# One exponential for two score banks in an attention and FP4 feed-forward kernel

## What is computed

```python
h = layernorm(x) * (1 + ca) + sa
q, k, v = h @ Wq + bq, h @ Wk + bk, h @ Wv + bv        # 16 heads of 16
scores = einsum('bhqd,bhkd->bhqk', q / 4, k) + 8 * rel_bias[bucket]
ctx = einsum('bhqk,bhkd->bhqd', softmax(scores), v)
x = x + ga * (ctx @ Wo + bo)
h = layernorm(x) * (1 + cb) + sb
x = x + gb * fp4_linear(silu(fp4_linear(h, w_gate)) * fp4_linear(h, w_up), w_down)
```

## Time and profile before

| | |
|---|---|
| median of three runs | 3792.81 us |
| lowest and highest | 3792.51 and 3795.49 us |
| span of the profiled execution | 3785.4 us |
| TensorE busy | 3473.1 us, 92% |
| TensorE weight loads | 2040.4 us |
| VectorE busy | 3208.1 us, 85% |
| ScalarE busy | 1872.9 us, 49% |
| GpSimd busy | 1696.3 us, 45% |
| mean granted TensorE clock | 0.968 |

### The profile page before, as it was taken

The page is one execution under the profiler, slowest core; times in us unless marked ns, Lnnn a source line. Parts: engine busy times, 40 slices in busy tenths (PEclk is TensorE's granted clock), DMA queues, the critical chain, the costliest instruction groups (busy, mean ns, idle before and its releaser), DMA issues.

```text
span 3785.4 us, 81397 instructions
## 1 busy us (share of the span) xinstructions
PE 3473.1 (92%) x22906; PEld 2040.4 (54%) x22906; DVE 3208.1 (85%) x7270; ACT 1872.9 (49%) x3800; POOL 1696.3 (45%) x1773
## 2 busy tenths in 40 slices
PE   1699999999999999999999999999999999999986
PEld 0245555555555555555555555555555555555554
DVE  7468888888888888888888888888888888888976
ACT  2265555545555455555554555555455545555541
POOL 2214544445454444444444445444445444444454
PEclk6799999999999999999999999999999999999997
DMA  3543323233332323332323432323333232333000
GB/s 98 97 83 70 73 50 67 50 65 74 73 62 59 58 54 73 75 73 50 67 46 69 74 72 59 59 56 60 72 73 65 60 55 53 73 75 66 20 22 12
DMA packets 199199, 237.30 MB, mean 63 GB/s; under 512 B 23424, under 2 KB 177568, under 8 KB 198736
## 3 DMA queue, kind: packets, MB, share of 16 engines
q1 hardware_dynamic: 198736, 231.64, 31.3%
HBM read 163.72 MB, written 67.31 MB: 61 GB/s over the span
## 4 chain that ended last, share of the span: by engine, by line
issue 46%; POOL 29%; PE 14%; DVE 6%; POOLq 2%; DMA 2%; SPq 1%; ACT 1%; DVEq 0%; ACTq 0%
POOL hidden L1250 5%; POOL hidden L1248 5%; PE ps_x L630 4%; POOL hidden L1274 4%; POOL parts L1219 3%; POOL proj L1212 3%; PE ps_o L618 2%; PE rings L581 2%; POOL ffn_in L1262 2%; POOL x_mid L1243 2%; POOL rstd L1260 2%; PE rings L597 1%; PE ps_x L656 1%; POOL hidden L1252 1%; POOLq L122 1%
## 5 line engine op out<-in xcount | busy, mean ns | idle before, releaser
L779 ACT ACTIVATE probs<-rings 128x512 f32<-128x512 f32 x2048 | 1208.2, 600 | 997.1 <-PE rings L584 964.5
L975 DVE TENSOR_REDUCE neg_max<-rings 128x1 f32<-128x512 f32 x2048 | 1366.0, 679 | 209.9 <-PE rings L600 205.0
L581 PE MATMUL rings<-q_rows,k_rows 121*128 121x512 bf16 x2048 | 797.6, 390 | 19.1 <-ACT probs L779 9.8
L597 PE MATMUL rings<-k_rows,q_rows 120*128 120x512 bf16 x2048 | 788.1, 385 | 28.4 <-DVE neg_max L975 17.4
L618 PE MATMUL ps_o<-probs,values 128*32 128x512 f32 x4096 | 545.9, 605 | 18.8 <-ACT probs L779 18.8
L581 PEld LDWEIGHTS rings<-q_rows,k_rows 121*128 121x128 bf16 x2048 | 200.3, 98 | 603.3 <-issue 400.2
L600 PE MATMUL rings<-band_m,rev 128*128 128x192 f16 (+1 forms) x2048 | 496.6, 242 | 0.0
L582 PE MATMUL rings<-band_t,rev 128*128 128x128 f16 x2048 | 454.2, 222 | 0.0
L1274 POOL TENSOR_TENSOR hidden<-hidden,inv 128x704 f32<-128x704 f32 x128 | 177.9, 1390 | 598.5 <-DVE inv L1038 598.5
L584 PE MATMUL rings<-band_t,rev 128*128 128x128 f16 (+1 forms) x2048 | 434.1, 212 | 0.0
L840 ACT ACTIVATE tanh<-ps_x 128x256 f32<-128x256 f32 (+1 forms) x384 | 140.4, 365 | 451.1 <-PE ps_x L630 451.1
(11 more groups left out here) (180 smaller groups left out, 6815.0 us busy)
## 6 DMA issues: line engine op xcount, KB each, us to landing
parts_dram<-parts SPq DMA_DIRECT2D x128, 384.0 KB, 2.3
q_rows<-parts_dram SPq DMA_DIRECT2D x384, 128.0 KB, 4.5
k_rows<-parts_dram SPq DMA_DIRECT2D x384, 128.0 KB, 7.0
mod_rows<-mod_rows_dram SPq DMA_DIRECT2D x32, 640.0 KB, 5.3
x_in<-in_x SPq DMA_DIRECT2D x32, 512.0 KB, 8.8
x_mid<-in_x SPq DMA_DIRECT2D x128, 128.0 KB, 2.1
out<-x_mid SPq DMA_DIRECT2D x128, 128.0 KB, 1.7
probs<-in_wmod SPq DMA_DIRECT2D x1, 1536.0 KB, 8.0
```

The lines of the kernel that those rows point to most:

```text
L581: mm(ps_s[:, bank, :], kr[0:ROW_MAX + 1, h, k0:k0 + P], qr[0:ROW_MAX + 1, h, :], start=True, stop=False)
L597: mm(ps_m[:, bank, :], q_rows[par][0:ROW_MAX, h, j * P:(j + 1) * P], k_rows[par][0:ROW_MAX, h, :], start=True, stop=False)
L779: A(prob(s, j), ps_s[:, (4 * s + j) % RING_S, :], ACT.Exp).then_inc(exp_done, 1)
L975: v.tensor_reduce(neg_max[:, par, 4 * h + j:4 * h + j + 1], ps_m[:, (4 * h + j) % RING_M, :], AX.X, ALU.max, negate=True).then_inc(max_don ...
```

## The change

The two score banks are filled one right after the other, in quarters 0 and 2, and one exponential of 128 x 1024 reads both and writes two neighbouring slices of `probs` (`prob_pair`). `exp_done` counts pairs, 32 for a batch. The first score product of a pair waits for the pair before it, the second waits for nothing. ScalarE issues the exponential only in quarters 0 and 2, with the two waits for `scores_ready` and `pv_done` ahead of each. The jobs, the max products and the context product stay in their quarters.

```diff
+        def prob_pair(unit, j):
+
+            at = 2 * (unit % 2) if j < 2 else 4
+            return probs[:, at:at + 2, :]
...
-                at = 4 * s + j
-                bank = at % RING_S
+                bank = j % RING_S
                 if s % 8 == 0 and j == 0:
                     wait(pe, max_placed[s // 8], 16 * (it.n + 1))
-                wait(pe, exp_done, it.n * 64 + ring_freed(at, RING_S))
+                if bank == 0:
+                    wait(pe, exp_done, it.n * 32 + 2 * s + j // 2)
...
-                wait(pe, exp_done, prev * 64 + 4 * (u + 1))
+                wait(pe, exp_done, prev * 32 + 2 * (u + 1))
...
-                        if it.has(0):
+                        if j % 2 == 0 and it.has(0):
                             scores(it, s, j)
+                            scores(it, s, j + 1)
...
-                        if it.has(0):
-                            e = n * 64 + (4 * s + j)
-                            wait(act, scores_ready, e + 1)
+                        if j % 2 == 0 and it.has(0):
+                            wait(act, scores_ready, n * 64 + (4 * s + j) + 2)
                             if j == 0:
                                 wait(act, pv_done, n * 16 + (s - 1))
                             if j == 2:
                                 wait(act, pv_done, n * 16 + s)
-                            A(prob(s, j), ps_s[:, (4 * s + j) % RING_S, :], ACT.Exp).then_inc(exp_done, 1)
+                            A(prob_pair(s, j), ps_s, ACT.Exp).then_inc(exp_done, 1)
```

## The result

The changed kernel takes 3768.15 us, the median of five runs (3763.27 to 3775.49), against 3792.51 us for the kernel before in five runs on the same chip (3778.47 to 3795.49). The ratio is 0.9945, with a 95% interval of 0.9928 to 0.9962: faster by 0.55%. The forecast of 3779 was 11 us too high, on the right side. The profiled execution has a span of 3773.3 us and a time of 3775.49; it is the slowest of the five, so sums from this trace are some 7 us above the median. In the five runs of the changed kernel the time is 2.1 or 2.2 us longer than the span, so the profiled execution of the kernel before, of which only the span of 3785.4 is known, took an estimated 3787.6, less than the median. The spans therefore show a gain of 12 us where the medians show 24.

The account below looks back on a forecast made before the run. TensorE and VectorE were taken to bound the kernel by turns, not ScalarE. Terms of −0.62 us over some 29 batches (−18) and +4 for the last gave −14 on 3785.4, plus 7.4 from span to median: 3779 us, range 3748 to 3818.

Parts of the forecast that it names:

- Reading the bound: ScalarE isn't the bound; a cheaper exponential is worth nothing by itself, TensorE or VectorE sets the time by place.
- The pair's price, 1.04 us: One 1024-wide exponential on ScalarE takes 1.04 us against 1.08 to 1.30 for two; 100 us saved, off the path.
- Slot 12, −0.57 and −0.20: Context product no longer waits 0.57 us for an exponential queued behind p3's copies; wo product starts 0.20 earlier.
- Slot 5, −0.40: A score product moves ahead of oT's wait into TensorE's idle time: 0.31 us at full pace, 0.6 at half.
- The gaps: TensorE waits for the pair 0.6 us after slot 3, 0.7 after slot 15; VectorE's lag swallows both; 0.05 elsewhere.
- Rival 1: The gaps count in full: +1.03 us a batch, +34 us, 3827 (half of it 3810); chance 0.24.
- hq_h, +0.25 twice: ScalarE's hq_h copy comes behind the pair, delaying VectorE's hq_l: +0.25 us for slots 2 to 4, +0.25 for slot 14.
- The first ones have spare time.: The first batches lose nothing to gaps, unlike the last batch, where eight boundaries cost +4 us.
- Rival 2: VectorE binds from slot 12 to the branch, gains there don't pass on: −0.1 us a batch, 3794; chance 0.24.
- Rival 3: TensorE's clock stays at 2.4 GHz behind slot 5's waits, 1.7 us less per affected batch: 3750; chance 0.10.
- behind slot 3 or 15: Sign of being wrong: new half-clock stretches of TensorE at these places.
- the 110.3 named as a check: Sign of being wrong: a batch that isn't 110.3 us long; one batch before took 110.93.

Follow-up runs that it names:

- split: Changed kernel, but each score bank is read by its own exponential of 512, so that a bank comes free on its own; 3748.44 us, ratio 0.9882.
- p3_later: Kernel before, with ScalarE's two copies of projection p3 issued one quarter later, behind the exponential of slot 11's quarter 3; 3768.12 us, ratio 0.9949.
- slot5: Kernel before, with the score product of slot 5's quarter 3 issued a quarter earlier, ahead of the oT job; 3773.24 us, ratio 0.9967.
- hybrid: Changed kernel, but in quarters 2 and 3 of slots 3 and 15 the two banks are read by separate exponentials; 3760.29 us, ratio 0.9934.
- split_hq: Changed kernel with one exponential per bank, and ScalarE copying hq_h between those of quarters 0 and 1 in slots 2, 6, 10, 14; 3742.73 us, ratio 0.9894.
- both: Kernel before with two edits: p3's copies a quarter later, and the score product of slot 5's quarter 3 a quarter earlier; 3754.34 us, ratio 0.9918.

## Why the prediction was right, and where it wasn't

The forecast was 14 us gained; the profiled spans show 12, the medians 24, the ratio 21 of 3792. The range of 3748 to 3818 held the time. Term by term:

- **Reading the bound.** That a cheaper exponential is worth nothing and TensorE's banks and VectorE's lag decide was right: ScalarE lost 98.3 us of work (100 forecast), and `split`, which gives the saving up, is the faster kernel.
- **The pair's price, 1.04 us.** Measured 1025 ns as the mean of 1024, 1.02 in the loop. The Trainium skill, page "ScalarE: Activation LUTs", section "What ACT_TABLE_LOAD costs", by which it would be an estimated 1.04, was 1.5% high. The overlap of some 93 ns between neighbours that it gives there is 0.11 us here (two exponentials of 0.60, 0.49 from start to start).
- **Slot 12, −0.57 and −0.20.** Right in size and in effect: the wait went from 18.8 to 0.9 us in all (0.57 × 29 = 16.5 forecast), and `p3_later`, which takes only this one away, brought 19.3 us. Wo of slot 12 starts 0.06 us after the max matmul ahead of it instead of 0.26, the forecast's 0.20. Together with slot 0's gap the two give the −0.51 of the table for slots 12 to 0. The context product of slot 12 in the changed kernel starts without a wait, where the earlier trace rows has 0.57:

```profile
1994.70 0.39 PE L685 MATMUL ps_x<-ident,context 128*128 128x128 f32 x2
1995.01 1.06 PE L623 MATMUL ps_o<-probs,values 128*32 128x512 f32 x8
```

- **Slot 5, −0.40.** Right in the total: `slot5` alone brought 12.5 us, 0.43 a batch. The forecast took 0.31 us at full clock and 0.6 at half and went between. At half clock it was 0.57; at full clock it was nothing in `slot5` and 0.12 to 0.20 with the whole change. So the term hangs on the half clock that before has in 21 of 24 batches. In the changed kernel oT waits 0.25 instead of 0.58 and takes 0.66 instead of 0.81:

```profile
1949.29 0.66 PE L679 MATMUL ps_x<-ident,o_t 128*128 128x128 f32 x4 [0.25 <-DVE hidden L1117]
```

- **The gaps.** Their places and sizes were right: 0.64 us at slot 4 (0.6 forecast). At slot 0 the first score product starts 0.83 us after the matmul ahead of it in every second batch, where before has 0.10: 0.73 (0.7 forecast), of which the rows count 0.59 as idle. In the other batches, behind the branch, it is 1.70 against 1.69, swallowed as forecast. At slots 8 and 12 of the loop there is no wait. What failed is the sentence that VectorE's lag swallows both. The one at slot 0 passes through to the end of its stretch: slots 12 to 0 are 0.33 us longer than in `split`, and VectorE's 2 us at the branch didn't cover it. The way from slot 0 to xT0 is 0.22 us longer than in `split` in the mean, but not in most batches: without a half-clock stretch in slots 0 to 4 it takes 39.78 us in the changed kernel (20 batches) and 39.95 in `split` (21). So there slot 4's gap was swallowed, and some of slot 0's too. The four batches with the half clock behind slot 2 take 42.42. Rival 1 was right that the gaps cost something, 0.52 us a batch and 12.3 us over the 24, but most of it came by way of the clock, in four batches, and not as the bare gap that rival 1 adds up; `hybrid` shows that it goes with the two gaps.
- **hq_h, +0.25 twice.** 0.38 at slot 2, or some 0.28 without `split`'s batch 12, and nothing at slot 14 by the traces of `split` and `split_hq`, against 0.50 forecast; the timed runs don't confirm even that.
- **"The first ones have spare time."** Wrong. Batches 0 to 2 have quarters without jobs, like the last batch, and 14 waits for the pair opened there, at nine different slots. Against the kernel before, as the forecast counts, batches 0 to 4 took 3.2 us longer and all that comes behind batch 28 3.4 (forecast: 0 and +4); against `split`, which has the order's gains there too, 6.7 and 6.0. One such wait in the first batch and one in the last, in the timeline of TensorE:

```profile
185.97 0.39 PE L586 MATMUL rings<-q_rows,k_rows 121*128 121x512 bf16 x1 [0.54 <-ACT probs L784]
...
3588.08 0.39 PE L586 MATMUL rings<-q_rows,k_rows 121*128 121x512 bf16 x1 [1.01 <-ACT probs L784]
```

- **The sum.** The two gains made 31 us (`both`), 34 forecast. The costs made 10 us by after against `both`; the forecast had 20, too much for hq_h and too little for the gaps and the first batches. By the spans, where after's profiled execution was a slow one, the two are 36 and 24 us. Not in the forecast were a gain of 0.14 us a batch in slots 8 to 12 and two costs, the half clock behind slot 2 and the first batches. So the total was near for a reason that is partly luck: terms missed on both sides. Against `split` instead of `both` the costs are 24 us (by the ratios) and the order's gain 45; which of the two is the better ledger hangs on the 14 us by which `split` and `both` differ in their ratios and which their traces (2.7 us) don't show.
- **Rivals.** Rival 1 would have needed all gaps to pass on; what they cost is told above. Its sum also counts hq_h once where the forecast counts it twice, and leaves out the forecast's 0.20 and 0.40. Rival 2 fell with `p3_later`. Rival 3's step happened in part, 10 half-clock stretches behind slot 5 instead of 22. At 0.46 us each (20.54 less 20.08) the 11 fewer of the 24 batches are worth 5 us, not the 1.7 each that rival 3 took, and the four new ones behind slot 2 took 10 us back. The forecast had named new ones "behind slot 3 or 15" as a sign of being wrong; it left them out of its sum. A batch takes 111.44 us, 0.79 less than before, where 0.62 was forecast; the 110.3 named as a check was taken from a batch shorter than the mean of 112.23.

The kernels that beat both are `split` and `split_hq`, at 0.9882 and 0.9894, the same within their intervals: the new order with one exponential for each bank.

## What to carry to other kernels

Where a change both reorders issue and widens an instruction, build the two halves apart: here the order was worth −1.2%, the wide read took 0.6% back, and the wide read with the old order cost 9.5%. The 0.6% isn't a constant of the wide read either: with slot 5 filled it is gone. A wide instruction over two buffers saves its engine little (0.06 us of 1.08) and holds the first buffer 0.42 us longer, so look at every place between two such reads, in the first and last iterations too, for what the filling engine still has to do. And before a whole schedule is rewritten, find the few places where a queue holds someone up: two of them gave 1.32 of the 1.65 us a batch that the reordering gave in the loop. Last, read a mean over batches batch by batch: four of 24 carried most of what the pair cost.
